# A perceiver block on one core: the wave kernel evaluated and split once per lag and spread by transfers, and the first iterations and the drain of the attention loop in another order

## The reference, cut to what matters

```python
h = layernorm(x)                                     # (16, 64, 512)
x = x + cross_attention(h, ctx)                      # per row only the 32 largest scores are kept
# wave attention over the tokens, 16 heads of 32, B*T = 1024 tokens
deposit = (elu(k) + 1) * v                           # k, v, q, gate from layernorm(x)
t = arange(1024)
kern = exp(-softplus(damp) * t) * cos(freq * t + phase)     # per head
kern = kern / sum(abs(kern))                         # over all 1024 lags
conv = causal_convolution(deposit, kern)             # of length 64 in each sequence
out  = (elu(q) + 1) * (coupling @ conv) * sigmoid(gate)
x = x + out @ Wout.T + bout
x = x + W2t @ gelu(W1t @ layernorm(x) + b1) + b2     # ternary weights
```

## Time and profile before

| | |
|---|---|
| median of 3 runs | 466.33 us (465.85 to 466.46) |
| profiled execution | 466.23 us, of which the span of its instructions is 464.5 us |
| busy, PE / DVE / ACT / POOL | 96% / 70% / 55% / 49% of the span |
| loop, iterations 0 / 1 / 2 / 3 (PE, from its first chunk) | 13.7 / 17.5 / 20.3 / 18.1 us |
| loop, iterations 4 to 7, each | 16.65 us |

### The profile page before, as it was taken

How to read it: one execution, slowest core, us unless ns; L and a number is a source line. 1 busy time by engine, 2 the same in 40 slices (tenths; PEclk the granted TensorE clock), 3 DMA queues, 4 the chain that set the end, 5 groups by cost and what they waited for, 6 DMA issues and landing times.

```text
span 464.5 us, 6292 instructions
## 1 busy us (share of the span) xinstructions
PE 447.9 (96%) x2146; PEld 352.8 (76%) x2146; DVE 326.9 (70%) x594; ACT 253.3 (55%) x392; POOL 226.2 (49%) x265
## 2 busy tenths in 40 slices
PE   6999989899999999889999999999999999999996
PEld 2588655588888888678888888888788888888884
DVE  4899679699999999978998893655872223522224
ACT  1777949577878887765787446443541221111111
POOL 6703098497779777834001761334226643333330
PEclk9999999999999999999999999999999999999999
DMA  7997733253444342570880300000000000100002
GB/s 222 414 370 286 260 105 113 69 159 122 127 138 131 118 117 90 182 226 1 338 289 11 110 1 23 1 0 0 2 0 0 1 0 1 68 23 1 0 1 91
DMA packets 23327, 48.94 MB, mean 105 GB/s; under 512 B 2688, under 2 KB 2688, under 8 KB 22272
## 3 DMA queue, kind: packets, MB, share of 16 engines
q1 hardware_dynamic: 23296, 48.55, 30.8%
HBM read 46.44 MB, written 2.10 MB: 105 GB/s over the span
## 4 chain that ended last, share of the span: by engine, by line
PE 67%; DVE 19%; ACT 5%; issue 4%; POOL 2%; DMA 2%; DVEq 0%; SPq 0%; ACTq 0%
PE bank L1250 10%; PE bank L1252 10%; PE bank L1251 10%; PE bank L1697 6%; PE bank L1699 6%; PE bank L1683 6%; PE bank L1684 6%; DVE mt_lo L1005 4%; PE bank L1265 4%; DVE work L1018 3%; DVE mx L1014 3%; PE bank L1257 2%; POOL nat_lo L428 2%; PE bank L1343 2%; DVE s_t L1025 1%
## 5 line engine op out<-in xcount | busy, mean ns | idle before, releaser
L428 POOL TENSOR_TENSOR nat_lo<-ctxr,nat_hi 128x512 fp32r<-128x512 f32 x64 | 83.9, 1338 | 21.0 <-ACT nat_hi L612 20.6
L801 ACT ACTIVATE g<-bank,b1c 128x512 f32<-128x512 f32 x32 | 22.1, 689 | 92.2 <-PE bank L1699 92.2
L1230 DVE CAST g_hi<-g 128x512 fp32r<-128x512 f32 x32 | 13.9, 434 | 74.9 <-ACT g L801 74.8
L483 POOL TENSOR_SCALAR w2s<-w2t 128x512 fp32r<-128x512 int8 x32 | 19.9, 621 | 65.9 <-PE bank L1684 65.9
L1697 PE MATMUL bank<-xt_lo,w1s 128*128 128x512 f32 x128 | 50.8, 397 | 0.0
L1699 PE MATMUL bank<-xt_hi,w1s 128*128 128x512 f32 x128 | 50.7, 396 | 0.0
L1683 PE MATMUL bank<-w2s,g_lo 128*128 128x512 f32 x128 | 50.2, 392 | 0.2 <-DVE g_lo L1232 0.2
L1684 PE MATMUL bank<-w2s,g_hi 128*128 128x512 f32 x128 | 50.2, 392 | 0.0
L588 ACT ACTIVATE mt_hi<-bank 128x512 fp32r<-128x512 f32 x64 | 37.8, 595 | 18.6 <-PE bank L1423 18.2
L1005 DVE TENSOR_TENSOR mt_lo<-bank,mt_hi 128x512 fp32r<-128x512 f32 x64 | 43.5, 681 | 4.7 <-ACT mt_hi L588 4.4
L1423 PEld LDWEIGHTS bank<-ident,ctxr 128*128 128x128 f32 x256 | 30.5, 141 | 12.9 <-issue 4.9
(11 more groups left out here) (234 smaller groups left out, 1205.8 us busy)
## 6 DMA issues: line engine op xcount, KB each, us to landing
ctxr<-ctx SPq DMA_DIRECT2D x64, 256.0 KB, 2.8
wab<-w1T SPq DMA_DIRECT2D x4, 1024.0 KB, 10.4
wab<-w2T SPq DMA_DIRECT2D x4, 1024.0 KB, 5.7
wgraw<-wgT SPq DMA_DIRECT2D x4, 1024.0 KB, 5.3
wst<-w1T SPq DMA_DIRECT2D x4, 1024.0 KB, 7.6
wst<-w2T SPq DMA_DIRECT2D x4, 1024.0 KB, 7.1
resid<-x SPq DMA_DIRECT2D x4, 512.0 KB, 6.3
out<-resid SPq DMA_DIRECT2D x8, 256.0 KB, 2.2
```

The costliest lines, as they stand in the source:

```text
L428: pool.tensor_tensor(nat_lo[:, par, c, :], ctxr[:, b % 4, c, :], f(nat_hi[:, par, c, :]), ALU.subtract).then_inc(nat_lo_ok, 1)
```

## The change

It does these things:

- **Wave kernel by lag.** CT becomes NC + 1 = 9: 8 columns for the norm and one whose row p holds lag 63 - p. `klag` [128, 16] replaces `kern`. After scaling by the norm it is turned by PE (in `totals`) to one row per head, split by DVE into `lag_hi` and `lag_lo` in `scales`, and stored by four transfers into `lags` in HBM, with 64 zeros behind each row. After the last v product four transfers read it back into the two factors: partition p of a quarter reads 64 values from position p on, for each of 16 heads. The triangles now lie off the diagonal with their columns reversed, so `wave` reads its bank backwards. The work of POOL and DVE on `kern`, `toe_hi` and `toe_lo` goes, but for the four fills with zeros.
- **The start.** `x_bias` becomes four row sums on DVE and one product with ones; it, `coupling` and `norms` stand between the last q products, each with a bank of its own. All eight `token_part`s come before the loop. DVE makes `turns` instead of POOL. The absolute sums begin earlier (seven before the loop), and wv is loaded two sums earlier.
- **Iterations 0 to 3.** `wvo_step(0)` moves into iteration 0; `nat_hi` and `nat_lo` of sequence 0 move from iteration 1 to 0; `turn_prob(0)` stands before `wvo_step(3, (2, 3))` instead of behind `wvo_step(3)`; `attn_bias` is one tile at the end of each iteration on POOL.
- **The drain.** Iteration 8 has its own ACT list; pair 6's `amt` uses other buffers and its projection another bank, so that `project(6)` runs in iteration 8 around `turn_prob(7)`; `wk` is split in halves and `k_product(0)` stands before the turns of tiles 4 and 5.

```diff
-CT = T + NC
+CT = NC + 1
+        def amt_part(pair, low):
+            if pair == NT - 2:
+                return qs[:, 2 * low:2 * low + 2, :, :].rearrange("p c b n -> p (c b n)")
+            return (amt_lo if low else amt_hi)[:, :]
+        def att_bank(pair):
+            return bank[1 if pair == NT - 2 else 6]
+        lags = nc.dram_tensor("lags", (2, H, 2 * T), F32, kind="Internal").ap()
 # SP
                 if b == 1:
                     for k in range(3, 2 * DC):
+                        if k == 2 * DC - 2:
+                            sp.dma_start(wvraw[:, :, :], rows(wv)).then_inc(wv_in, 16)
                         abs_load(k)
-                    sp.dma_start(wvraw[:, :, :], rows(wv)).then_inc(wv_in, 16)
+                if b == 4:
+                    sp.wait_ge(lag_ok, 2)
+                    sp.wait_ge(tpos_ok, 5)
+                    for m, part in enumerate((lag_hi, lag_lo)):
+                        sp.dma_start(lags[m, :, T:2 * T], lag_none[0:H, :]).then_inc(lag_put, 16)
+                        sp.dma_start(lags[m, :, 0:T], f(part[0:H, :])).then_inc(lag_put, 16)
...
             sp.wait_ge(v_ps, NT)
+            sp.wait_ge(lag_put, 64)
+            for m, part in enumerate((toe_hi, toe_lo)):
+                shifted = bass.AP(tensor=lags.tensor, offset=m * H * 2 * T, ap=[[1, T], [2 * T, H], [1, T]])
+                for q in range(2):
+                    sp.dma_start(f(part[q * T:q * T + T, :, (1 - q) * T:(1 - q) * T + T]),
+                                 shifted).then_inc(toe_in, 16)
             sp.dma_start(woutraw[:, :, :], rows(woutT)).then_inc(wout_in, 16)
             sp.dma_start(bias_o[:, :], bout.partition_broadcast(P)).then_inc(bout_in, 16)
 # POOL
-                nat_lo_part(i - 1, 0)
+                if i != 1:
+                    nat_lo_part(max(i - 1, 0), 0)
                 split_q(i + 1, 0)
-                if i == 0:
-                    attn_bias(range(NT))
                 nat_lo_part(i - 1, 1)
+                attn_bias(i - 1)
-            pool.wait_ge(norm_ok, 1)
-            pool.tensor_tensor(kern[:, :, :], kern[:, :, :], ...)
-            for q in range(2):
-                pool.affine_select(out=k, in_=k, ...)
 # ACT
+                if i == NT:
+                    cross(NT - 1, 1)
+                    nat_hi_part(NT - 1, 0, (0, 1))
+                    am_part(NT - 2, 0)
+                    nat_hi_part(NT - 1, 0, (2, 3))
+                    am_part(NT - 2, 1)
+                    keep_exp(NT - 1)
+                    amt_hi_part(NT - 2)
+                    nat_hi_part(NT - 1, 1, (0, 1))
+                    nat_hi_part(NT - 1, 1, (2, 3))
+                    continue
...
-            split_hi(2, wgq_hi[:, :, :])
+            split_hi(2, wgq_hi, 0, DC)
             am_part(NT - 1, 0)
-            ln2_apply(4)
-            split_hi(0, wk_hi[:, :, :])
+            split_hi(0, wk_hi, 0, DC // 2)
             am_part(NT - 1, 1)
-            ln2_apply(5)
+            split_hi(0, wk_hi, DC // 2, DC)
             amt_hi_part(NT - 1)
+            ln2_apply(4)
+            ln2_apply(5)
 # DVE, before the loop
+            def xbias_sum():
+                for o in range(DC):
+                    row_sum(sum_k, woraw, 2, o).then_inc(sums_ok, 1)
+                    dve.wait_ge(sums_ok, DC + o + 1)
+            xbias_sum()
+            token_part(6)
+            token_part(7)
+            mix_part()
+            token_part(0)
+            xbias_part()
+            token_part(1)
+            dve.wait_ge(cos_ok, 2)
+            dve.tensor_tensor(klag[:, :], ...)      # targ * tdec, 16 wide; then habs, 128 wide
+            token_part(2)
+            token_part(3)
+            norm_part()
+            token_part(4)
+            token_part(5)
 # DVE, in scales(), and in the wave
+                dve.tensor_copy(lag_hi[0:H, :], spread).then_inc(lag_ok, 1)
+                dve.tensor_tensor(lag_lo[0:H, :], spread, f(lag_hi[0:H, :]), ALU.subtract).then_inc(lag_ok, 1)
-                if n in (1, 3):
-                    dve.tensor_copy(toe_hi[s, :, s], kern[s, :, :]).then_inc(toe_hi_ok, 1)
-                    dve.tensor_tensor(toe_lo[s, :, s], kern[s, :, :], f(toe_hi[s, :, s]), ...)
+                back = bank[2 + n % 2][:, :].rearrange("p (k t) -> p k t", k=4)[:, :, ::-1]
 # PE
+            def totals():
+                pe.transpose(bank[5][0:H, T:2 * T], klag[0:T, :], ident[0:T, 0:T])
+                pe.matmul(bank[5][:, 0:2 * DC], ones[:, :].to_broadcast([P, P]), wabs[:, :], ...)
             def wvo_in_turn(i, j):
+                if i == 0 and 4 <= j:
+                    wvo_step(0, (j - 4,))
                 if i == 1:
                     if j == 0:
+                        totals()
+                    elif j in (2, 3):
+                        wvo_step(1, (2 * j - 4, 2 * j - 3))
+                    elif j >= 4:
+                        wvo_step(2, (j - 4,))
                 if i == 2 and j < 2:
                     wvo_step(3, (2 * j, 2 * j + 1))
+            for n in range(3, 2 * DC):
+                if n == 5:
+                    coupling()
+                if n == 6:
+                    x_bias()
+                if n == 7:
+                    norms()
+                q_product(n)
...
                 score(g0 + 1 - ahead)
-                wvo_in_turn(i, 1)
                 if i == 2:
                     turn_prob(0)
+                wvo_in_turn(i, 1)
...
                     join(i - 2, 0)
+                    join(i - 2, 1)
                     project(i - 3, (2, 3))
-                    join(i - 2, 1)
+                    project(i - 2, (0, 1))
                     turn_prob(i - 1)
+                    project(i - 2, (2, 3))
                     continue
...
-            project(6, (0, 1))
             for par in range(2):
                 weigh(7, par, 0)
                 weigh(7, par, 1)
             join(7, 0)
-            project(6, (2, 3))
             join(7, 1)
+            k_product(0)
             ln2_turn(4)
             ln2_turn(5)
-            k_product(0)
             project(7, (0, 1, 2, 3))
-            pe.wait_ge(toe_lo_ok, 2)
+            pe.wait_ge(toe_in, 64)
```

More of the change, by code:

```diff
@@ L1 @@
 from contextlib import ExitStack
-from concourse import mybir
+from concourse import bass, mybir
 F32 = mybir.dt.float32
@@ L82, in perceiver_kernel @@
             [("wvraw", [P, DC, D], F32), ("woraw", [P, DC, D], F32)])
-        kern = sb("kern", [P, H, T])
+        klag = sb("klag", [P, H])
+        lag_hi = sb("lag_hi", [P, T], F32R)
+        lag_lo = sb("lag_lo", [P, T], F32R)
+        lag_none = sb("lag_none", [P, T])
         rnorm = sb("rnorm", [P, H])
@@ L144, in perceiver_kernel @@
          (cvt_hi, cvt_lo, gate, bias_2, w1s, w2s, g32, g_hi, g_lo),
-         (wab, turns)) = region(
+         (wab, turns, sum_k, sum_q, bias_x)) = region(
             [("wvo_hi", [P, DC, D], F32R), ("wvo_lo", [P, DC, D], F32R),
@@ L385, in _ @@
                                     ALU.mult))
-            link(pool.tensor_tensor(targ[:, :, :], targ[:, :, :], bc(wpar[:, 2, :]), ALU.add))
+            pool.tensor_tensor(targ[:, :, :], targ[:, :, :], bc(wpar[:, 2, :]), ALU.add).then_inc(tpos_ok, 1)
             def rstd(n):
@@ L397, in _, with attn_bias @@
                 rstd(t)
-            link(pool.tensor_scalar(turns[:, :, :], targ[:, :, :], 1.0 / TWO_PI, ROUND, ALU.mult, ALU.add))
-            pool.tensor_scalar(turns[:, :, :], turns[:, :, :], -ROUND, 1.0, ALU.add, ALU.mult).then_inc(turns_ok, 1)
-            def attn_bias(ts):
-                for t in ts:
+            def attn_bias(t):
+                if 0 <= t < NT:
                     pool.wait_ge(xbias_ok, 1)
                     pool.wait_ge(ln_ready, t + 1)
-                    pool.tensor_tensor(resid[:, t, :], resid[:, t, :], bias_x[:, :], ALU.add).then_inc(xres_ok, 1)
+                    pool.tensor_tensor(resid[:, t, :], resid[:, t, :], xn[:, 1, :], ALU.add).then_inc(xres_ok, 1)
             def split_q(pair, b):
@@ L921, in token_part @@
                 dve.wait_ge(u_ps, 1)
-                if t:
-                    dve.wait_ge(ctok_sum, t)
+                if t != 6:
+                    dve.wait_ge(ctok_sum, (t + 2) % NT)
                 dve.scalar_tensor_tensor(out=sum_q[:, :], in0=bank[5][:, :], scalar=1.0, in1=first_xn(t),
                                          op0=ALU.mult, op1=ALU.mult, accum_out=ctok[:, t:t + 1]).then_inc(ctok_sum, 1)
-            for t in range(4):
-                token_part(t)
-            dve.wait_ge(cos_ok, 2)
-            dve.tensor_tensor(kern[:, :, :], targ[:, :, 0:T], tdec[:, :, 0:T], ALU.mult).then_inc(kern_ok, 1)
-            dve.tensor_tensor(habs[:, :, :], targ[:, :, T:CT], tdec[:, :, T:CT], ALU.mult).then_inc(kern_ok, 1)
-            dve.wait_ge(kern_ok, 2)
-            absolute(habs[:, :, :], habs[:, :, :]).then_inc(kern_ok, 1)
+            def xbias_sum():
+                dve.wait_ge(wo_in, 16)
+                dve.wait_ge(qbias_ok, 1)
```

(36 more changed lines are left out.)

253 lines of the change are left out of this document (111 added, 142 removed).

## The result

The changed kernel takes 459.89 us (median of four runs, 459.57 to 461.01) against 466.38 for the kernel before on the same chip: a ratio of 0.9863, 95% interval 0.9844 to 0.9882. That is 6.5 us faster. It is inside the range for 8 in 10 (453.0 to 461.0), but 4.2 us short of the forecast of 455.7, and outside the likeliest case's own range (453.5 to 457.5). Four more executions of the same program gave 0.9867 (0.9852 to 0.9882).

What follows compares the result with a forecast made beforehand. PE was taken as full early and at the end, with gaps in the head and drain, and DVE setting iterations 4 to 7. Gains 7.5 + 2.6 + 0.4 = 10.5 us from 466.2 gave 455.7; 8-in-10 range 453.0 to 461.0.

Steps and rivals of the forecast that it cites:

- two weaker cases: Rivals: the head gives 5 us, time 458.2 (chance 0.18); the drain gives nothing, time 458.3 (chance 0.08).
- the head: Start to iteration 4 on DVE: fewer PE gaps and an earlier at_lo(0) were to gain 7.5 us.
- the drain: Iteration 8 to project(7): filled PE waits and an earlier k_product(0) were to gain 2.6 us, bounds 0 and 3.5.
- the first chunk of iteration 2 at 73.6: In the head: PE was to reach iteration 2 at 73.6 instead of 79.4 us.
- head two-thirds: Rival: DVE late before iteration 0, which takes 11.5 us; the head gives 5, time 458.2; chance 0.18.
- It keeps the same list, so the whole head gives 7.5: From at_lo(0) to 117.76 DVE's work was taken as unchanged, so the 7.5 us gained by at_lo(0) would remain.
- PE fills its waits with `project(6)`: In the drain: project(6) moves wholly ahead of weigh(7), filling PE's waits for amt_lo (0.78 us) and the probabilities.
- so `at_lo(7)` stays where it is: In iteration 8: DVE does amt_lo(6), 0.6 us, before the probabilities, not after, leaving at_lo(7) unmoved and weigh(7) at 196.1.
- the work that leaves POOL there, the scaling and cutting of `kern`, is longer than the add that comes: Argument against the rival that the drain gives nothing because POOL or ACT replaces the wait (458.3 us, chance 0.08).
- The convolution and the tail: At the convolution: removing DVE and POOL work on toe and kern was to gain 0.4 us, range 0 to 0.5.
- The spread: Four transfers reading lags back before the convolution: 39 ns a packet, 9.9 us, hidden; free up to 15.2 us.
- rival "late": Spread at 60 to 100 ns a packet delays bias_o and DVE's first cvt_lo: 456 to 466 us; chance 0.08.

Runs made afterwards that it cites:

- DVE loaded: Changed kernel with six more 128x512 operations on DVE between its first two token operations, writing an unread scratch tile: 462.25 us, ratio 0.9914 to the kernel before.
- the old order: Changed kernel with iteration 8 and drain in the order of the kernel before on PE, DVE, ACT and SP: 463.37 us, ratio 0.9929 to the kernel before.

## Why the prediction was right in direction and too large

The range held because it reached over two weaker cases, and neither of them came as described: the head gave more than two thirds, the drain more than nothing. Four stretches each fell short, by 1.0, 0.8, 1.6 and 0.9 us.

**The head: 6.5 of 7.5 us.** By intervals it is 6.8, the rest the chance of the start. The step "the first chunk of iteration 2 at 73.6" failed by 1.1: 50.21 for 49.7, 9.83 for 9.6 and 14.64 for 14.3, three small sums each too short. The step from there to `at_lo(0)` was right (5.3 forecast, 5.26 measured), and the price of turning the probabilities first (1.7) was shown by undoing it. That DVE would just be in time was right, and loading it showed how little more would have broken it. The rival "head two-thirds" named a true limit that was not reached. Undone one at a time, the early turning is worth 1.65 us and `wvo_step(0)` in iteration 0 1.75. That `x_bias` became one product among the q products was not undone by a run of its own, so its share is not shown. DVE was 5.3 ahead in iteration 1 by the forecast; it was 4.17 (`mt_lo(2)` at 64.89 for 69.06).

**"It keeps the same list, so the whole head gives 7.5": a loss of 0.8.** I held the loop fixed at its pace of DVE. It is so, 16.65 us, as long as the context is there. In every changed kernel one to three context loads came late, 0.12 to 1.14 us each, mostly in iterations 3 and 6, where the kernel before has only one of 0.13 behind its 0.45 at 79.42. The loss of the loop follows them: in twelve of the thirteen changed kernels the sum of these waits and the loss against 97.34 agree within 0.3 us (0.79 and 0.78 in the changed one, 2.15 and 2.07 where a load was 1.14 late). The forecast had left out how thin this cover was. The last load for iteration 3 landed at 99.24 before, 0.5 us ahead of PE's chunk at 99.7; now it lands at 93.51 and the chunk starts at 93.55. Counted from its start, iteration 2 is 1.5 us shorter, and the load, which waits in it for `nat_lo` to free the buffer, came only 1.0 sooner. Where the probabilities are turned late iteration 2 is longer again, and this wait is gone. In iteration 6 it is the transfer that is slower: the last load took 4.1 us from issue to landing where 2.4 to 3.1 are common. Why is not shown; taking POOL's adds out did not remove these waits.

**The drain: 1.0 of 2.6.** This is the term that failed most. "PE fills its waits with `project(6)`" came true, and all three waits went (2.6 us, just the forecast's sum). Two other steps failed.

The first is "so `at_lo(7)` stays where it is". It came 12.6 us behind `at_lo(6)`, where it was 10.7 before: with `amt_lo(6)` ahead of the probabilities DVE waits 0.54 for ACT, and the masking took 1.80 us and not 0.98. So `weigh(7)`, which was forecast 12.3 behind `at_lo(6)` as before (196.1 - 183.8), started 13.3 behind: 1.0 us. The nine profiles with this order of DVE have 12.6, the others, with the probabilities first, 10.7.

The second is what follows `weigh(7)`. To have `project(6)` early, the two `join`s came to stand next to each other, and the second needs ACT to copy the other half of `am` through the one tile `amsb`, which the first must have read: 0.75 us. The kernel before had projection steps between them as cover. I costed the moved step by the wait it fills and not by the wait it had been covering. From the start of `weigh(7)` to `k_product(0)` it took 6.4 us. The forecast had 6.0, of which 0.6 was a wait for `wk_lo` that PE did not meet. The same wait at the first pair of joins seems to cost little, as `weigh(7)` stands behind `at_lo(7)` anyway.

Steps put back between the last pair alone gave nothing (PE waited for `at_lo(7)`); together with the probabilities first they give 1.2 us, so that 2.3 of 2.6 are there to be had. How the 1.2 divide between the two is not shown, as the probabilities first were never run alone. Also the argument that "the work that leaves POOL there, the scaling and cutting of `kern`, is longer than the add that comes" was wrong in kind: the add comes ahead of the statistics and costs the old order 2.8 us, and only the new order of iteration 8 and the drain hides it.

**The convolution and the tail: -0.5 for 0.4.** The two short gaps are still there (0.25 and 0.42 us between starts, before 0.28 and 0.43), though the four toe operations are gone from DVE: these were not their cause. Of the 0.5 us that are lost instead, 0.4 stands in the trace as one wait for `xt_lo` behind the wave, where before had none; the rest is spread over many matmuls.

```profile
324.44 0.63 PE L1298 MATMUL bank<-ident,xn 128*128 128x128 f32 x4 [0.43 <-DVE xt_lo L869]
```

I ran nothing on it. The wait stands in every changed kernel but one, the one with DVE loaded, whose edit is 280 us earlier; its cause stays open.

**The spread: hidden, as forecast.** 26.5 ns a packet (0.81 x 16 x 8.5 us over 4160) against 39; they cost what the 64-byte packets did and not what lies between by size. The Trainium skill's page DMA: Bandwidth & Descriptors (section Specifications) gives 512 bytes as the least size of a transfer for line rate. The trace agrees that 256 bytes fall short of it: its packets moved 1.05 MB between 248.96 and 254.99, 174 GB/s, where the large ones had 357. That is near the forecast's estimate by half the rate, 5.9 us. The rival "late" would have worked otherwise than I wrote: the convolution gives way first, 22.3 us behind the first issue (the forecast's 22.2), and POOL's adds, which I had called the tighter limit, did not stop PE even when they ended at 285.9. The issues were dearer than thought: 0.7 to 1.1 us each and not 0.43.

## What to carry to other kernels

A step that is moved leaves a hole where it stood: before moving it into a wait, read which round trip it covered, above all where two steps share one staging tile. And read which engine the filled wait leads to: where DVE's `at_lo(7)` set the start of `weigh(7)`, a hole filled on PE only moved the wait. And a small operation that is put on an idle engine must be priced by what queues behind it there in the drain, where the order of four engines is one chain: here the same add cost nothing in one order of iteration 8 and the drain, and 2.8 us in the other. Compare intervals inside the traces, not absolute starts, where less than 1 us is at stake.

## What the hardware showed that I had not expected

- PE's granted clock fell behind waits of 2.66 us (to 0.61 over the next 3 us, then 0.82) and of 2.94 us (0.83 over ten), and did not fall behind 1.45. In the first case this made a wait 1.2 us longer than before into a loss of 2.8 us.
- Copies of 256 bytes that re-read 16 KB of memory 64 times over cost 26.5 ns a packet, as 64-byte ones do, and issuing one of these transfers (1024 packets) took SP 0.7 to 1.1 us.
- The same masking of the probabilities on DVE took 0.92, 0.98 and 1.80 us in three orders of iteration 8, with POOL's `nat_lo` beside it in all three. What makes the difference was not tried.
